# State-space stage: two of four tile sums added by accumulating transfers instead of GpSimd, and two softplus steps moved from VectorE to GpSimd

## The reference, cut to what matters

```python
delta = jax.nn.softplus(dt @ W_dt.T + b_dt)
dA = jnp.exp(delta[..., None] * A)
dBx = delta[..., None] * Bm[:, :, None, :] * xc[..., None]

def step(h, t):
    dA_t, dBx_t, C_t = t
    h = dA_t * h + dBx_t
    return (h, jnp.einsum('ben,bn->be', h, C_t))
_, ys = jax.lax.scan(step, h0, (dA..., dBx..., Cm...))
y = ys.transpose(1, 0, 2) + D_skip * xc
y = y * jax.nn.silu(z)
return y @ W_out.T
```

## Time and profile before

| | |
|---|---|
| median of 3 runs | 2458.88 us (2457.44 to 2459.68) |
| the profiled execution | 2460.9 us, its span 2459.2 us |
| mean granted TensorE clock | 0.866 |
| busy in the span | PE 1911.8, PEld 1465.2, DVE 1678.1, ACT 1184.7, POOL 1515.8 us |
| state-space stage | from about 2 us to 1157.5 us of the span |

### The profile page before, as it was taken

How to read it: one execution, slowest core, us unless ns; L and a number is a source line. 1 busy time by engine, 2 the same in 40 slices (tenths; PEclk the granted TensorE clock), 3 DMA queues, 4 the chain that set the end, 5 groups by cost and what they waited for, 6 DMA issues and landing times. The chain is left out here.

```text
span 2459.2 us, 35798 instructions
## 1 busy us (share of the span) xinstructions
PE 1911.8 (78%) x10252; PEld 1465.2 (60%) x10253; DVE 1678.1 (68%) x3193; ACT 1184.7 (48%) x2021; POOL 1515.8 (62%) x1152
## 2 busy tenths in 40 slices
PE   6787879686979787875599999907877784799970
PEld 2445455554555454544499999904655664699970
DVE  1779898989989898985644444437634897644438
ACT  2677777777777767773232222226632441111112
POOL 1799999999999999994133333335622420355532
PEclk9888979798989888887699999958988896799995
DMA  3111111111101011112411111142000014122226
GB/s 123 38 35 40 39 37 36 39 39 37 39 23 52 27 49 31 43 36 77 165 48 47 47 48 48 41 139 77 9 18 11 9 35 163 42 71 70 70 65 192
DMA packets 76780, 138.63 MB, mean 56 GB/s; under 512 B 10369, under 2 KB 47873, under 8 KB 75858
## 3 DMA queue, kind: packets, MB, share of 16 engines
q1 hardware_dynamic: 62994, 99.67, 12.4%
q0 software_dynamic: 13632, 37.24, 4.8%
HBM read 104.86 MB, written 32.01 MB: 56 GB/s over the span
## 5 line engine op out<-in xcount | busy, mean ns | idle before, releaser
L787 DVE TENSOR_TENSOR_SCAN a_hs<-a_dA,a_carry,a_hs 128x512 f32<-128x512 f32 x512 | 628.3, 1264 | 63.5 <-ACT a_dA L559 53.7
L399 POOL TENSOR_TENSOR a_hs<-a_u,a_b_bc 128x1024 f32<-128x1024 f32 (+1 forms) x292 | 634.9, 2182 | 2.3 <-POOL a_u L381 1.9
L929 PE MATMUL a_h_ps<-k_ident,a_hs 128*128 128x128 f32 x2064 | 328.3, 308 | 174.7 <-DVE a_acc L750 95.6
L929 PEld LDWEIGHTS a_h_ps<-k_ident,a_hs 128*128 128x128 f32 x2064 | 268.4, 158 | 293.5 <-DVE a_hs L787 86.2
L559 ACT ACTIVATE a_dA<-a_delta,a_a_neg 128x512 f32<-128x512 f32 x512 | 350.1, 687 | 39.6 <-DVE a_hs L787 38.4
L411 POOL TENSOR_TENSOR a_acc<-a_acc,a_part 128x512 f32<-128x512 f32 x242 | 331.7, 1371 | 28.6 <-ACT a_part L573 28.3
L573 ACT ACTIVATE a_part<-a_h_ps,a_c_tok 128x512 f32<-128x512 f32 x242 | 166.0, 686 | 203.8 <-PE a_h_ps L929 176.0
L1229 POOL DMA_INDIRECT expert_rows<-m0e_ys,k_pair x71 | 78.7, 1109 | 232.5 <-DVE m0e_ys L1285 221.6
L750 DVE SCALAR_TENSOR_TENSOR a_acc<-a_h_ps,a_c_tok,a_acc 128x512 f32<-128x512 f32 x242 | 176.3, 728 | 46.5 <-PE a_h_ps L929 46.4
L863 PE MATMUL a_fx<-a_hT,a_w_x 128*128 128x512 f32 x432 | 200.9, 597 | 2.2 <-ACT a_halo L495 1.4
L1295 DVE TENSOR_TENSOR m0e_hT<-m0e_gs,m0e_u 128x512 f32<-128x512 f32 x70 | 48.2, 688 | 191.5 <-ACT m0e_gs L1248 191.5
(11 more groups left out here) (420 smaller groups left out, 3793.2 us busy)
## 6 DMA issues: line engine op xcount, KB each, us to landing
a_b_bc<-b_rows SPq DMA_DIRECT2D x132, 256.0 KB, 3.2
c_y<-expert_rows SPq DMA_DIRECT2D x16, 512.0 KB, 5.6
q_y<-expert_rows SPq DMA_DIRECT2D x16, 512.0 KB, 5.9
norm_rows<-a_x SPq DMA_DIRECT2D x9, 512.0 KB, 3.3
m0w_up<-in_m_up SPq DMA_DIRECT2D x1, 4096.0 KB, 12.1
m0w_gate<-in_m_gate SPq DMA_DIRECT2D x1, 4096.0 KB, 22.2
m0w_down<-in_m_down SPq DMA_DIRECT2D x1, 4096.0 KB, 32.1
c_xl<-in_L_attn_x SPq DMA_DIRECT2D x8, 512.0 KB, 3.7
```

The costliest lines, as they stand in the source:

```text
L399: last = pool.tensor_tensor(hs[k][:, w, :], u[s][:, w, :], b_bc[:, k:k + 1, :].broadcast_to([P, width, T]), ALU.mult)
L787: dve.tensor_tensor_scan(hs[k][:, c, :], dA[c][:], hs[k][:, c, :], carry[:, hf, c, n:n + 1], ALU.mult, ALU.add).then_inc(s_scan, 1)
L929: last = pe.transpose(hT_ps[j % 2][:, c * P:(c + 1) * P], hs[(n - 1) % NBUF][:, c, j * P:(j + 1) * P], ident[:])
```

## The change

GpSimd's two additions in each iteration become one transfer that it issues, which adds `part` (both tiles, 512 KB) into `acc`. `part` gets a second buffer, and so the transfer of one iteration may still be reading while ACT fills the other. Each transfer is issued only after the one before has landed. ACT's weighting waits for the landing of the transfer two iterations back. PE's `y0` waits for the landing of the last transfer of the unit. Softplus's subtraction and addition go from DVE to GpSimd: the subtraction at the end of its iteration 12, the addition in 13, ahead of u. `hn` becomes the same memory as `x1`, and so the normalisation waits for the last store of `x1`; ACT also waits for the subtraction in iteration 14. At the start two transfers that add zeros are issued and waited for, after one more fill.

```diff
-        hn = m.sb("hn", [P, TJ, D])
+        hn = x1
-        part = m.sb("part", [P, TJ // 2, ED])
+        part = m.sb("part", [P, 2, TJ // 2, ED])
...
-        def added_count(U, n, j):
-
-            return lin(U, ADDS, NO * (n - 1 if n > 1 else 0) + OFF.index(j) + 1 + NO)
+        def added_count(U, n, back=0):
+
+            return lin(U, 16 * ADDS, 16 * ((n - 1 if n > 1 else 0) + 3 - back))
...
             pool.memset(z[1][:], 0.0).then_inc(s_prep, 1)
-            pool.memset(acc[1][:], 0.0).then_inc(s_prep, 1)
+            pool.memset(acc[1][:], 0.0).then_inc(s_const, 1)
             pool.memset(xc[1][:], 0.0).then_inc(s_prep, 1)
-            pool.sem_inc(s_add, NO)
-            pool.wait_ge(s_const, 2)
+            pool.memset(part[:], 0.0).then_inc(s_const, 1)
+            pool.wait_ge(s_const, 4)
+            pool.sem_inc(s_prep, 1)
+            for k in range(2):
+                pool.dma_start(acc[1][:, OFF[0]:TJ:2, :], part[:, k], accum_op=ALU.add).then_inc(s_add, 16)
+                pool.wait_ge(s_add, 16 * (k + 1))
...
+            def softplus_sub(F, s):
+
+                for q in range(2):
+                    pool.wait_ge(s_fix, lin(F, 2, q + 1))
+                    pool.tensor_tensor(flat(delta[s], q), flat(delta[s], q), flat(acc[s], q), ALU.subtract).then_inc(s_sub, 1)
+
+            def softplus_add(F, s, q):
+
+                pool.wait_ge(s_ln, lin(F, 1, 1))
+                pool.wait_ge(s_sub, lin(F, 2, q + 1))
+                pool.tensor_tensor(flat(delta[s], q), flat(delta[s], q), flat(u[s], q), ALU.add).then_inc(s_delta, 1)
...
-            def add(U, n, j, s):
-
-                if j not in OFF or n == 1:
-                    return
-                pool.wait_ge(s_part, part_count(U, n, j))
-                if n == 0:
-                    pool.wait_ge(s_add, added_count(U, 0, j) + -NO)
-                elif n > 2:
-                    pool.wait_ge(s_add, added_count(U, n - 1, j))
-                pool.tensor_tensor(acc[s][:, j, :], acc[s][:, j, :], part[:, j // 2, :], ALU.add).then_inc(s_add, 1)
+            def add(U, n, s):
+
+                if n == 1:
+                    return
+                pool.wait_ge(s_part, part_count(U, n, OFF[-1]))
+                pool.wait_ge(s_add, added_count(U, n, 1))
+                pool.sem_inc(s_go, 1)
+                pool.dma_start(acc[s][:, OFF[0]:TJ:2, :], part[:, n % 2], accum_op=ALU.add).then_inc(s_add, 16)
...
                         for q in range(2):
                             product(U, ahead, q, hf if ahead < NS else 1 - hf)
-                            add(U, n, 2 * q + 1, hf if n else 1 - hf)
+                        add(U, n, hf if n else 1 - hf)
                         if n == 14:
                             rms(tile0, lambda per_: lin(U, per_, per_))
+                        if n == NS - 4:
+                            softplus_sub(F, 1 - hf)
                         if n == NS - 3:
...
                             for q in range(2):
+                                softplus_add(F, 1 - hf, q)
+                            for q in range(2):
                                 front_u(F, 1 - hf, q)
...
-                    act.wait_ge(s_add, added_count(U, 0, j) + -NO if n == 0 else added_count(U, n - 1, j))
-                    to = part[:, j // 2, :]
+                    if j == OFF[0]:
+                        act.wait_ge(s_add, added_count(U, n - 2) if n > 3 else added_count(U, 0, (2, None, 0, 1)[n]))
+                    to = part[:, n % 2, j // 2, :]
...
                         if n == 1:
+                            act.wait_ge(s_rst, lin(U, 16, 16))
                             act.wait_ge(s_pw, lin(F, 1, 1))
                         if n == 14:
+                            act.wait_ge(s_sub, lin(F, 2, 2))
...
-                            act.wait_ge(s_rst, lin(U, 16, 16))
...
-                        if n == 13:
-                            softplus_add(F, 1 - hf)
...
                         if n == 12:
-                            softplus_sub(F, 1 - hf)
...
                     if whole == "y0":
                         pe.wait_ge(s_acc, lin(U, NS * ND, 2 * ND))
-                        pe.wait_ge(s_add, lin(U, ADDS, 2 * NO))
+                        pe.wait_ge(s_add, added_count(U, 0))
```

More of the change, by code:

```diff
@@ L225, in mamba_phase @@
         s_part = m.sem("weighted_by_act")
-        s_add = m.sem("summed_by_pool")
+        s_add = m.sem("summed_by_transfers")
+        s_go = m.sem("ready_to_sum")
         s_carry = m.sem("carry")
@@ L258, in mamba_phase @@
         ON = tuple(j for j in range(TJ) if j not in OFF)
-        ND, NO, ADDS = len(ON), len(OFF), len(OFF) * (NS - 1)
+        ND, NO, ADDS = len(ON), len(OFF), NS - 1
         def count(name, U):
@@ L381, in front_u, with flat @@
                 pool.tensor_tensor(u[s][:, half, :], delta[s][:, half, :], xc[s][:, half, :], ALU.mult).then_inc(s_u, 1)
+            def flat(t, q):
+                return t[:].rearrange("p a b -> p (a b)")[:, q * 2 * T:(q + 1) * 2 * T]
+            def softplus_sub(F, s):
[6 more added lines that the diff above has]
+                pool.tensor_tensor(flat(delta[s], q), flat(delta[s], q), flat(u[s], q), ALU.add).then_inc(s_delta, 1)
             def rms(tile0, nth):
@@ L415, in _ @@
             pool.wait_ge(s_xc, 1)
+            softplus_sub(F0, 0)
             for q in range(2):
+                softplus_add(F0, 0, q)
                 front_u(F0, 0, q)
@@ L448, in _ @@
                             for q in range(2):
+                                softplus_add(F, 1 - hf, q)
+                            for q in range(2):
                                 front_u(F, 1 - hf, q)
             end = (0, 2 * NB, None)
-            for j in OFF:
-                add(end, 0, j, 1)
+            add(end, 0, 1)
             rms(TILES - TJ, lambda per_: per_ * (2 * NB + 1))
@@ L692, in softplus_fix @@
                                              op0=ALU.add, op1=ALU.subtract).then_inc(s_fix, 1)
-            def softplus_sub(F, s):
-                for q in range(2):
-                    dve.wait_ge(s_fix, lin(F, 2, q + 1))
-                    dve.tensor_tensor(flat(delta[s], q), flat(delta[s], q), flat(acc[s], q), ALU.subtract).then_inc(s_sub, 1)
-            def softplus_add(F, s):
-                dve.wait_ge(s_ln, lin(F, 1, 1))
-                for q in range(2):
-                    dve.wait_ge(s_sub, lin(F, 2, q + 1))
-                    dve.tensor_tensor(flat(delta[s], q), flat(delta[s], q), flat(u[s], q), ALU.add).then_inc(s_delta, 1)
             def gated(U, c, s):
@@ L766, in _ @@
             softplus_fix(F0, 0)
-            softplus_sub(F0, 0)
-            softplus_add(F0, 0)
             dve.wait_ge(s_free[side("ct")], FSEQ[side("ct")].index("ct") + 1)
@@ L954, in _ @@
             pe.wait_ge(s_acc, lin(end, NS * ND, 2 * ND))
-            pe.wait_ge(s_add, lin(end, ADDS, 2 * NO))
+            pe.wait_ge(s_add, added_count(end, 0))
             pe.wait_ge(s_da, 2 * NB * NS * EC + EC)
```

## The result

The changed kernel takes **2518.86 us** (median of 4 runs, 2517.16 to 2521.7) against 2459.28 for the kernel before on the same chip (4 runs, 2457.44 to 2462.64): a ratio of 1.0242, 95% interval 1.0224 to 1.026. It is slower by 59.6 us, where the prediction had 2497, 38 us more. The profiled execution took 2517.93 us, its span 2516.2, 57.0 more than the 2459.2 of before. Times within a stage are taken from the two profiled executions.

What follows compares the result with a forecast made beforehand. The prediction saw a ring of stretches with different limits, TensorE filling the convolution, and y0 newly waiting for the last landing. Seven units 13.3, start 8.8, first unit 6.4, end 9.4: +38 us, 2497; range 2447 to 2560.

Steps and rivals of the forecast that it cites:

- The ring: One unit, 129.6 us: fix, GpSimd's row to its power, ACT's norms, y0 and f0, convolution, silus, fix, following each other.
- d: Time GpSimd spends issuing one accumulating transfer: taken as 1.3 us, between 0.97 or less and 2.1.
- L: Time from an accumulating transfer's issue to its landing: estimated 6.3 us, ends 3.3 and 9.
- 4d + L - 9.95: Lengthening of a unit in us when L is under 4.65 + d; otherwise 3d + 2L - 14.6.
- The unit: Each unit +1.9 us: y0, waiting for the last landing, comes 3.5 later, less 0.9 and 0.65 given back.
- The give-back behind y0: Small waits for hn and hT, and for f1 and its copy, vanish behind y0: 0.9 us back per unit.
- The 0.65 before the silus: ACT's weighting in iteration 8 no longer waits 1.23 us for GpSimd, so the silus start some 0.65 us earlier.
- Start: One more fill, two zero transfers in turn, then power and norms: f0 at 26.0 instead of 17.25, +8.8 us.
- First unit: GpSimd's row after VectorE's fix, then transfer 0 landing at 104.6 against y0 at 96.59: +6.4 us.
- Busy time as the bound: Rival: GpSimd's 16 us and VectorE's 8.9 us relief per unit arrive in full, 2386 us; chance 0.05.
- Short transfers: Rival: L under 4.65 + d, sum 31d + 12L - 80; shorter still gives 2449 or about 2431; chance 0.13.
- Transfers longer than an iteration: Rival: above L = 7.7 transfers queue in iterations 2 to 12 and engines wait; 2560 to about 2655; chance 0.13.

Runs made afterwards that it cites:

- 5: Changed kernel with the unit's last two sums made by GpSimd additions instead of a transfer, power ahead of them, product 18 behind: 2493.22 us, ratio 1.0141.
- 8: Changed kernel with plain transfers that overwrite instead of adding (output not the layer's, only its time counts): 2487.46 us, ratio 1.011.
- 4: Changed kernel with GpSimd's rms of iteration 14 moved ahead of product 16: 2526.09 us, ratio 1.0272.
- 12: Changed kernel with only one more wait, GpSimd's product of iteration 12 starting behind VectorE's fix: 2517.82 us, ratio 1.025.
- 1: Changed kernel with the start's two zero transfers moved behind GpSimd's first power: 2503.09 us, ratio 1.0172.
- 9: Changed kernel with VectorE's softplus, late zero transfers, issue 13 behind u, GpSimd's last sums, plus product of iteration 12 waiting for the fix: 2429.14 us, ratio 0.9879.
- 6: Changed kernel with softplus back on VectorE, and the transfer of part 13 issued behind GpSimd's products for u: 2503.9 us, ratio 1.0187.

## Why the prediction was right, and where its sizes were off

- **Direction and mechanism: right.** The ring (fix, GpSimd's row, landing, y0, convolution) was read rightly. The convolution stayed at 43 us with TensorE full; GpSimd's saved 105 us bought nothing; y0 waits for an accumulating transfer in each unit; VectorE's saved time stands at the logits. Experiments 5, 8, 4 and 12 bear it out: no landing ahead of y0 (5), or shorter landings and issues (8), give units back; a VectorE that waits less at the logits (4) or has a shorter fix (12) doesn't.
- **d: right.** 1.2 us measured, 1.3 taken.
- **L: too high, and luckily so.** 5.2 us measured, 6.3 taken. The step's reasoning "reading the destination too is another 2.0" was near: the addition costs 1.8 (8). But the 1.0 for GpSimd's queue was wrong: its plain copy lands in 3.4 against SP's 3.2. By the prediction's own formula for such an L (4d + L - 9.95), d = 1.2 and L = 5.2 give a unit +0.05, not +1.9, and the whole sum (31d + 12L - 80) +20 instead of +38. With the right L the forecast would have been about 2478, 40 us short of the result instead of 22: the two errors had opposite signs.
- **The unit: +3.4 measured against +1.9, the step that was mis-sized.** Against the formula at the measured d and L it is +3.4 against +0.05. The formula let GpSimd start when part 12 is weighted and never wait again, and three waits say otherwise. The issue of 12 began 0.65 us behind its part (474.35 to 475.00). The issue of 13 waited 0.60 for its part. Transfer 15 took 6.87 us instead of 5.2, which held the last issue 1.55 us and with it everything behind. With 0.2 for the last landing (5.38) that is 2.9: in the unit shown y0 came 4.5 us later, where the formula with d = 1.2 and L = 5.2 has 1.6. The give-back behind y0 (0.9 forecast) was 0.2: y0 to the convolution took 8.35 us, before 8.57. The 0.65 before the silus came, as 0.70. Together they are the unit shown, 3.6 us longer (133.1 against 129.5).
- **The same gap in experiment 8.** There d = 0.74 and L = 3.4 give a unit -3.6 by the formula, and it measured -0.1. So the formula is 3.4 to 3.5 us short in both kernels; its constant was wrong, while the slopes held over this step.
- **Why transfer 15 is slow** can be read from what else was under way. In the changed kernel a transfer of sums lands in 5.05 us (median of 26) beside nothing, 5.2 (66) beside one load of B, 6.3 (13) beside two, and 7.1 (7, each a transfer 15) beside the store of x1 and loads of B. In the last unit no load of B follows; there transfer 15 goes out 1.99 us behind the store as ever and lands in 5.02. So the store alone doesn't slow it; the loads of B, or loads and store together, go with it. No run moved them.
- **Start: +16.3 against +8.8, the other term that was mis-sized.** Transfers beside the big loads were priced at 6.3 with 8 as a worse case; they landed in 10.3 and 8.9, with which the same sum gives +15.4. Experiment 1 took 13.7 of it back.
- **First unit +6.9 against +6.4, end +8.3 against +9.4**: close.
- **What I hadn't seen:** the fix. It was left as it was, 3.51 us, and took 6.59. In this kernel a shorter one gains nothing (12); in its neighbour with VectorE's softplus it decides (9). It is also why VectorE's busy time fell by 50 us and not by the 75 of the prediction's signs.
- **The other signs.** GpSimd is busy 110.9 of a unit's 133.1 us (83%), near the 80 named. f0 of the start runs at 33.70 and not at 26, by the start's landings. The sign against the forecast, waits of ACT for landings in iterations 4 to 12, seems to stand in the waits' rows, and isn't there: those seven end with PE's turn.
- **Rivals.** Busy time as the bound is refuted twice (5, 9: more GpSimd waits or work, less time). Short transfers: with 3.4 us of landing and 0.74 of issue the kernel is still at 2487, where the formula has about 2443; the start's landings (9.9 and 9.0 us) and the waits behind parts stay. Transfers longer than an iteration: the longest behind the start took 7.4 us and ACT waited for none in iterations 4 to 12; GpSimd's 23 waits for the landing before make 28.4 us in all.
- **Open.** Transfers without the softplus move, with short fixes, beat both kernels (9). Whether the transfers or the wait for the fix deserve the credit is open: the kernel before with the wait alone was not tried.

## What to carry to other kernels

Here, moving additions from an engine to transfers cost time as long as a consumer stood right behind the last one. What gave time back, in the runs of this kernel: the last sum of a chain on an engine (5, with a changed order), an issue behind the work that others wait for (6, little), and no wait for a landing while big loads are under way (1). An engine that becomes free earlier also starts earlier; look at what runs beside it then. The longest row of waits isn't the loss: removing VectorE's 5.6 us a unit (4) and its 4.2 us of lengthened fix (12) gave nothing, while 4.2 us at the same place gave 4.9 a unit, 38 in all, where VectorE was busy without a gap up to y0 (9). And a wait that a profile lays on a transfer is to be checked against when that transfer had to be there: a landing that merely falls into the same moment gets the name.

## What the runs showed of the hardware

- An accumulating 512 KB transfer within SBUF, issued by GpSimd, lands in 5.2 us (median; 5.0 to 7.4 behind the start) and takes 1.2 us to issue; the same without the addition 3.4 and 0.74 us, in two thirds of the packets (31600 against 47088). Beside two loads of 256 KB the accumulating one takes 6.3. Beside the loads of the start both take about 10 and 9 us.
- VectorE's fix reads two tiles in SBUF. Both halves take 2.36 us with nothing beside them. In the changed kernel, taken apart, the first half takes 5.45 us and ends 1.09 us behind the last of GpSimd's four pieces (467.71 to 473.10):

```profile
468.74 5.45 DVE L717 SCALAR_TENSOR_TENSOR a_acc<-a_acc,a_u 128x1024 f32<-128x1024 f32 x1 [1.09 <-ACT a_acc L571]
```

  In the kernel before they took turns: piece 1 ends at 439.13, the fix's first half at 440.22; piece 2 takes 2.25 us and ends at 441.34; the second half takes 2.29 and ends at 442.43. Each ends 1.1 us behind the other, so one waits until the other is through; they don't share. The Trainium skill has an exclusive lock on a port pair that VectorE and GpSimd share, and names a VectorE instruction with two SBUF inputs beside a GpSimd one that reads SBUF (SBUF — State Buffer, section on who interferes with whom). The rows agree with the wait. But in the changed kernel it lasted over four instructions of GpSimd, while in the kernel before VectorE got in after one. It isn't that the pieces overlap each other behind an accumulating issue (1.73 us each, started every 1.23): in experiment 8 they don't (1.27 us each), and the first half still takes 5.00 us. What decides whether VectorE gets in between isn't shown.
- The scans of VectorE, with one input in PSUM, weren't stretched beside GpSimd's work: 1249 to 1284 ns, all 512 of them.
